# A delta-rule pipeline whose four hand-written step sequences are replaced by newly drawn ones

## The reference, cut to what matters

```
q = silu(dwconv_causal(x @ Wq)); k = silu(dwconv_causal(x @ Wk)); v = silu(dwconv_causal(x @ Wv))
alpha = sigmoid(x @ Wa + ba);   beta = sigmoid(x @ Wb + bb)
def step(S, inp):                       # over the 1024 tokens, for each batch and head
    qt, kt, vt, at, bt = inp
    err = einsum('bhvk,bhk->bhv', S, kt) - vt
    S = at[..., None, None] * S - bt[..., None, None] * err[..., None] * kt[:, :, None, :]
    o = einsum('bhvk,bhk->bhv', S, qt)
    return (S, o)
o = layernorm(o) * ln_w + ln_b;  o = o * sigmoid(x @ Wg);  return o @ Wo
```

## Time and profile before

| | us |
|---|---|
| median of 3 runs | 1928.25 |
| lowest, highest | 1923.27, 1929.74 |
| the profiled execution | 1926.59 |
| its span in the trace | 1924.9 |

### The profile page before, as it was taken

How to read it: one execution, slowest core, us unless ns; L and a number is a source line. 1 busy time by engine, 2 the same in 40 slices (tenths; PEclk the granted TensorE clock), 3 DMA queues, 4 the chain that set the end, 5 groups by cost and what they waited for, 6 DMA issues and landing times.

```text
span 1924.9 us, 49241 instructions
## 1 busy us (share of the span) xinstructions
PE 1815.8 (94%) x19366; PEld 1345.0 (70%) x19366; DVE 1472.8 (77%) x2561; ACT 1308.0 (68%) x2850; POOL 945.0 (49%) x1890
## 2 busy tenths in 40 slices
PE   8899999998999789999999999999999999999687
PEld 4633333333778678888888888888888888887576
DVE  6699999992665468788788788888887887886365
ACT  2078888887343367777777777777777777776453
POOL 1234454444223426566556656556656656655133
PEclk9989999999999989999999999999999999999789
DMA  5201212111000201111011011111111111111001
GB/s 181 82 18 34 58 33 58 33 47 23 12 1 6 70 24 46 37 43 54 24 49 48 27 45 48 35 44 41 35 48 38 35 48 38 37 37 46 4 1 44
DMA packets 74133, 78.61 MB, mean 41 GB/s; under 512 B 13168, under 2 KB 60784, under 8 KB 73904
## 3 DMA queue, kind: packets, MB, share of 16 engines
q1 hardware_dynamic: 73904, 75.46, 13.2%
HBM read 66.13 MB, written 8.91 MB: 39 GB/s over the span
## 4 chain that ended last, share of the span: by engine, by line
PE 33%; DVE 15%; POOL 14%; issue 5%; ACT 1%; POOLq 0%; DVEq 0%; ACTq 0%
PE ps L1530 9%; DVE d_acc L1834 7%; POOL d_inv L1485 6%; PE ps L1560 6%; POOL d_term L1478 6%; PE ps L1581 2%; PE ps L1649 2%; DVE d_lane L1865 2%; PE ps L1631 2%; PE ps L1679 2%; DVE d_r_sb L1886 1%; PE ps L2009 1%; PE ps L1655 1%; PE ps L2023 1%; DVE d_ap L1851 1%
## 5 line engine op out<-in xcount | busy, mean ns | idle before, releaser
L1834 DVE SCALAR_TENSOR_TENSOR d_acc<-ps,d_par,d_acc 128x1023 f32<-128x1023 f32 (+2 forms) x288 | 365.8, 1270 | 41.4 <-ACT d_acc L1702 41.1
L601 ACT ACTIVATE a_prob<-ps 128x512 f32<-128x512 f32 (+2 forms) x640 | 309.3, 563 | 96.4 <-PE ps L567 91.3
L1530 PE MATMUL ps<-x1p,d_wh 128*128 128x512 f32 x1024 | 352.6, 426 | 9.5 <-DVE d_acc L1834 6.7
L623 DVE TENSOR_REDUCE a_mx<-ps 128x2 f32<-128x1024 f32 (+2 forms) x320 | 336.5, 1111 | 32.6 <-PE ps L551 25.5
L1702 ACT ACTIVATE d_acc<-ps,d_par 128x512 f32<-128x512 f32 x192 | 149.3, 778 | 106.5 <-PE ps L1530 103.4
L1530 PE MATMUL ps<-x1p,d_wl 128*128 128x512 f32 x512 | 203.4, 397 | 0.0
L1530 PEld LDWEIGHTS ps<-x1p,d_wh 128*128 128x128 f32 x1024 | 168.4, 191 | 35.9 <-DVE d_acc L1834 16.3
L510 POOL TENSOR_SCALAR_AFFINE_SELECT a_prob<-a_prob 128x128 f32<-128x128 f32 (+1 forms) x384 | 125.2, 330 | 123.6 <-ACT a_prob L601 112.8
L567 PE MATMUL ps<-q,k 51*128 51x512 bf16 (+2 forms) x640 | 174.6, 363 | 2.7 <-ACT a_prob L601 0.9
L581 PE MATMUL ps<-a_prob,a_v 128*32 128x512 f32 (+3 forms) x1536 | 164.3, 500 | 0.4 <-POOL a_prob L510 0.2
L546 PE MATMUL ps<-k,q 48*128 48x512 bf16 (+3 forms) x768 | 150.2, 338 | 9.5 <-DVE a_mx L623 7.4
(11 more groups left out here) (244 smaller groups left out, 4553.3 us busy)
## 6 DMA issues: line engine op xcount, KB each, us to landing
d_abc<-scratch_alpha SPq DMA_DIRECT2D x32, 512.0 KB, 3.9
d_gb<-scratch_g SPq DMA_DIRECT2D x32, 512.0 KB, 4.3
d_wr<-in_dw SPq DMA_DIRECT2D x16, 512.0 KB, 3.6
scratch_q<-p_parts SPq DMA_DIRECT2D x24, 128.0 KB, 2.4
q<-scratch_q SPq DMA_DIRECT2D x32, 96.0 KB
scratch_y<-a_oT SPq DMA_DIRECT2D x64, 36.0 KB
x_tok<-in_x SPq DMA_DIRECT2D x4, 512.0 KB, 7.6
q<-scratch_q SPq DMA_DIRECT2D x32, 64.0 KB
```

The lines of the kernel that those rows point to most:

```text
L601: inc(nc.scalar.activation(prob[:, y % PB, g:g + heads, off:], ps[:, PLACE["st", n, x], 0:heads * w].rearrange("p (h c) -> p h c", c=w), A ...
L623: inc(nc.vector.tensor_reduce(out, ps[:, bank:bank + 2, 0:heads * w].rearrange("p r (h c) -> p r h c", c=w), AX.X, ALU.max, negate=True), ...
L1530: last = nc.tensor.matmul(ps[:, bank, :], wp[g][:, k, i, :], x(part), start=(k == 0 and j == 0), stop=(k == KE - 1 and j == 2))
L1834: inc(nc.vector.scalar_tensor_tensor(acc[i][:, d:T], taps[:, 0:T - d], par[p][:, 4 * i + j:4 * i + j + 1], acc[i][:, d:T], ALU.mult, ALU.a ...
```

## The change

Nothing is computed in another way, no instruction of the steady stage is added or removed, and buffers and banks are as they were. All four sequences of `ORDER` are new, in order and in where the stage is cut. Two waits are added in `last_layer`'s function for DVE, on adds that earlier rows of DVE's own sequence make.

```
 ORDER = {
     "PE": """
...
-        O.w.7 S.z64 O.qs.7 O.pw.7 X.out.1 L.proj.2.0.0 S.y128 L.proj.2.0.1 L.proj.2.1.0 L.proj.2.1.1 S.z128 L.pair.0 S.w.0 L.pair.1 S.s.0 L.pair.2
...
+        X.out.1 O.w.7 S.z64 O.qs.7 O.pw.7 L.proj.2.0.0 L.proj.2.0.1 L.proj.2.1.0 S.y128 L.proj.2.1.1 L.pair.0 S.z128 L.pair.1 S.w.0 S.gate.0.0 S.s.0
...
     "POOL": """
-        X.wo S.solve.0 S.solve.1 S.solve.2 S.solve.3 S.solve.4 X.og.0 L.split X.og.1 L.scalars O.stats L.qg""",
+        S.solve.2 S.solve.3 S.solve.4 X.og.0 S.qg X.og.1 L.scalars O.stats L.split O.wo L.solve.0 L.solve.1""",
 }
...
     def ahead_vector(dve, step):
         if step == ("o_turn", 0):
             waits(dve, "gproj", 2)
+            waits(dve, "added", -2)
             w_norm.statistics(dve, 0)
             w_norm.normalise(dve, 0)
         if step == ("out", 0):
             for k in range(KE):
                 dve.wait_ge(x_high, k + 1)
                 nc.vector.tensor_tensor(xp[:, 0, 1, k, :], ps[:, k, :], plain(xp[:, 0, 0, k, :]), ALU.subtract).then_inc(x_low, 1)
+            waits(dve, "added", 0)
             w_norm.statistics(dve, 1)
```

More of the change, by code:

```diff
@@ L1244 @@
     "PE": """
[L1245 to L1248, removed]
@@ L1249 @@
-        E.proj.0.1.1 S.s.2 L.k_turn.0 S.gate.1.0 S.gate.1.1 S.pw.2""",
+        O.qs.5 O.w.5 L.proj.1.1.0 O.s.5 L.proj.1.1.1 O.ks.6 O.pw.5 S.y32 S.v_turn.1 O.w.6 S.z32 X.out.0 O.qs.6 O.s.6 O.pw.6 S.y64 S.k_turn.1 O.ks.7
+        X.out.1 O.w.7 S.z64 O.qs.7 O.pw.7 L.proj.2.0.0 L.proj.2.0.1 L.proj.2.1.0 S.y128 L.proj.2.1.1 L.pair.0 S.z128 L.pair.1 S.w.0 S.gate.0.0 S.s.0
+        S.gate.0.1 S.ks.1 S.pw.0 L.pair.2 L.pair.3 S.w.1 S.qs.1 E.proj.0.0.0 S.s.1 E.proj.0.0.1 S.ks.2 S.pw.1 E.proj.0.1.0 S.w.2 E.proj.0.1.1 S.qs.2
@@ L1250 @@
+        S.s.2 X.out.2 S.pw.2 S.ks.3 O.o_turn.0 X.out.3 S.w.3 L.v_turn.0 S.qs.3 S.s.3 S.pw.3 S.gate.1.0 S.ks.4 S.gate.1.1 L.k_turn.0 S.w.4 S.qs.4
+        O.o_turn.1 S.s.4 S.pw.4 E.proj.1.0.0 S.ks.5 E.proj.1.0.1""",
     "ACT": """
-        X.norm.0 O.pw.0 O.w.1 X.o_turn.0 O.pw.1 S.blocks X.norm.1 O.w.2 L.tap.0.0 L.tap.0.1 S.silu.2 O.pw.2 O.gate.1 O.w.3 X.o_turn.1 O.pw.3
-        S.v_turn.0 S.v_turn.1 O.w.4 L.tap.1.0 O.pw.4 O.w.5 S.spread X.og.0 X.og.1 S.y32 L.tap.1.1 O.pw.5 O.w.6 S.diag S.y64 O.pw.6 O.w.7 S.gate.0
@@ L1253 @@
-        S.z64 O.pw.7 L.silu.0 L.silu.1 S.y128 L.tap.2.0 L.tap.2.1 S.z128 S.w.0""",
+        X.pw.6 X.w.7 O.z64 X.pw.7 S.silu.0 S.silu.1 S.tap.2.0 O.y128 S.tap.2.1 O.z128 O.w.0 X.norm.0 O.gate.0 O.pw.0 O.w.1 S.silu.2 S.blocks L.tap.0.0
+        O.pw.1 O.w.2 X.norm.1 L.tap.0.1 O.pw.2 X.o_turn.0 O.w.3 S.v_turn.0 O.pw.3 O.gate.1 O.w.4 O.pw.4 X.og.0 X.o_turn.1 O.w.5 L.tap.1.0 S.spread
+        L.tap.1.1 S.y32 O.pw.5 O.w.6 S.v_turn.1 X.og.1 S.diag S.y64""",
     "DVE": """
-        O.s.3 L.conv.0.2 O.ks.4 X.o_turn.0 O.s.4 S.columns O.pw.2 O.ks.5 X.o_turn.1 S.turned O.s.5 S.k_turn.1 O.ks.6 O.pw.3 S.whole L.conv.1.0 O.s.6
@@ L1256 @@
-        X.out.0 O.ks.7 L.conv.1.1 O.pw.4 L.conv.1.2 O.pw.5 O.pw.6 O.pw.7 X.out.1 O.stats L.decay L.conv.2.0 L.pair.0 S.s.0 L.pair.1 L.pair.2 S.ks.1
-        L.pair.3 L.conv.2.1 S.s.1 L.conv.2.2 S.ks.2 L.lanes S.pw.0 S.pw.1 X.out.2 X.out.3 S.s.2 L.k_turn.0 E.conv.0.0 S.ks.3 E.conv.0.1""",
+        X.o_turn.0 O.s.4 O.pw.2 O.pw.3 O.ks.5 O.pw.4 S.k_turn.0 S.columns O.s.5 O.ks.6 X.o_turn.1 S.turned L.conv.1.0 O.pw.5 S.whole X.out.0 O.s.6
+        L.conv.1.1 O.ks.7 L.conv.1.2 O.pw.6 X.out.1 O.pw.7 O.stats S.k_turn.1 L.decay L.pair.0 L.conv.2.0 L.pair.1 S.s.0 L.conv.2.1 S.ks.1 L.conv.2.2
@@ L1258 @@
+        L.pair.2 L.pair.3 S.s.1 S.ks.2 S.pw.0 L.lanes S.s.2 X.out.2 S.ks.3 E.conv.0.0 X.out.3 S.pw.1 S.s.3 E.conv.0.1 S.ks.4 E.conv.0.2""",
     "POOL": """
-        X.wo S.solve.0 S.solve.1 S.solve.2 S.solve.3 S.solve.4 X.og.0 L.split X.og.1 L.scalars O.stats L.qg""",
+        S.solve.2 S.solve.3 S.solve.4 X.og.0 S.qg X.og.1 L.scalars O.stats L.split O.wo L.solve.0 L.solve.1""",
 }
```

## The result

The kernel with the new order takes 1972.85 us (median of 4 runs, 1971.74 to 1976.33), the kernel before 1928.99 us (median of 4, 1923.27 to 1932.58) beside it. The ratio is 1.0233, with a 95% interval of 1.0205 to 1.0262: slower by 44 us. I had predicted 1919 us, 1902 to 1938. The direction and the range are both wrong.

A forecast was written before the change was run, and what follows sets the result against it. It took the chain of waits from lanes through columns to lanes as the bound, with only columns to lanes movable: 30 x (-0.3) + 0 for the ends = -9 us, giving 1919 us, range 1902 to 1938.

The forecast's parts named there:

- Edits that I cost at nothing: POOL's qg moved between the two og, loads of alpha and g reissued on SP, two added waits: all priced at 0.
- the case without cover: If nothing hid POOL's moved qg, it would cost its 2.4 us per period.
- Rival 2: Slower by ACT's queue, if y128's copies end later than C+14.6: period 35.9, +15, 1943 us; chance 0.18.
- C: The start of columns in a period, from which the prediction counts the times of its steps in us.
- the tap: On ACT, one tap now ahead of y128's copies costs 0.7 us and gives back the 0.6 gained before.
- The walk: Step-by-step sum of the new order from columns to lanes, durations kept: period 35.08 us against 35.38, 0.3 less.
- The blocks: ACT's four blocks ahead of lanes, hidden before, are no longer hidden and cost 1.7 us per period.
- over a microsecond: Sign expected in the new trace: DVE idle that long ahead of lanes until ACT's blocks end.
- The ceiling: Most a new order could gain on PE by matmul busy time: 0.17 us per period, 5 us in all; not used.
- rival 3: Much faster, if PE stalls that the walk does not name go too: period shorter by 1.4, -42, 1886 us; chance 0.08.
- Ends: Pipeline fill (-1) and drain (-1.4 and +2.1 to +2.6): together 0, give or take 3 us.
- the late gating: In the drain, DVE's second gating comes ahead of the low parts PE's first up waits for: +2.1 to +2.6 us.

The follow-up runs named there:

- experiment 1: The kernel with the new order, with POOL's qg moved from between the two og to behind the second: 1889.03 us, ratio 0.9814 to the kernel before.
- experiment 2: The kernel before with one step moved, POOL's qg placed right behind solve.4: 1930.84 us, ratio 1.0039 to the kernel before.

## Why the prediction was wrong, step by step

**The step that failed** is "Edits that I cost at nothing". I costed the move of qg at nothing, with 2.4 us per period if its covers were gone, and looked for cover in semaphores only: who waits for qg, and whether the solve does. Nobody waits for it. It costs DVE 2.0 us per period by shutting out its gating, and PE 1.0 more through the clock, together 3.0 where I had put 0. The figure that I gave for the case without cover was near by luck; it came about in a way that was not among my rivals. Rival 2 has the same sign, and y128's copies do end beyond its C+14.6 in the kernel after (C+16.28). But it hangs on ACT's queue and the tap: here the 3.0 us come from DVE and the clock, and in experiment 1 the same queue of ACT ends them at C+13.30.

**The walk** was too cautious from its first step on. Experiment 1 is the order without the stall, and the kernel after in the period that starts at 1154.47 is the order with it; times are behind C:

| step | predicted | experiment 1 | after |
|---|---|---|---|
| whole's second transpose ends | 5.05 | 4.45 | 6.45 |
| ym ends | 8.1 | 7.50 | 9.50 |
| z64's first copy starts | 9.05 | 8.32 | 11.31 |
| y128's copies end | 14.0 | 13.30 | 16.28 |
| w_sb of chunk 0 starts | 16.0 to 16.5 | 15.45 | 18.44 |
| first state | 17.0 to 17.5 | 16.38 | 19.36 |
| lanes | 23.0 to 23.4 | 22.33 | 25.32 |

In the first rows experiment 1 is 0.6 us ahead of my walk, and 0.7 to 1.1 us at lanes: y32 starts at C+1.23 there (1017.14), where I had taken C+1.7. I had credited the new order with whole coming 0.6 sooner, and it was 1.2. From there on the durations between steps are mine to within 0.2 us, lanes included. (The middle of my C+23.0 to C+23.4 is 23.2, and I wrote 23.25; that is 1.5 us over the pipeline and changes nothing.) The column of the kernel after shows the failure entering at once: 2.0 in the first two rows, 3.0 from the third on, once y64 and what stands behind it up to z64 have run at half clock.

**The blocks** are exposed as I had said: DVE waits 0.21 to 0.26 us for them ahead of lanes, after 0.58 for PE's ks. I had named "over a microsecond" as the sign, which was wrong, because a state and an r_sb fill the rest. The chain of the kernel after does not pass over line 1732 either; from 1170 to 1192 it lies on PE's own row. So does nearly all of experiment 1's chain from 1027 on, and PE's row is busy for 34.02 of its 34.24 us. The walk of copies and lanes followed a string that is close to PE's own but was not shown to be the one that binds; what sets the 34.24 us stays open.

**The ceiling.** I had said that by matmul busy time the order could gain 0.17 us per period at most, and rightly did not use that. The gain was 1.2. Weight loads fell from 29.58 to 28.95 us in a period, matmuls from 34.99 to 34.02. So rival 3, the large gain with 0.08 of chance (a period shorter by 1.4 us), is where the kernel would have been but for qg: by the ratio of experiment 1 to the 1928.25 us of before it is 1892 us, against its 1886.

**Ends.** I had 0, give or take 3. From the first projection to the first columns it is 39.0 us (38.1 before), and the first period 39.3 (40.1 before). The tail behind the last columns is 151.8 us (153.6 before): sum -1.6. Of the parts, the time from the first to the last statistics of the last layer, in which the late gating lies, grew by 2.7 us (1824.6 to 1859.1, now 1871.8 to 1909.0), where I had +2.1 to +2.6 for that gating; the statistics come 4.3 us sooner behind the last columns, which I had at 1.4. In experiment 1 they come 8.1 us sooner and the tail is 147.8 us.

## What to carry over

When an instruction on POOL or DVE is moved, list what runs at its new place on the other of the two, and from where each takes its inputs: in the pairs of a DVE and a POOL instruction shown here that both read two operands from SBUF (gating and qg, scan and eps, gating and solve), the later one got through only behind the earlier, with no semaphore to show it. In a trace the sign is a group whose maximum is far above its median, or a tiny instruction that takes microseconds and ends when one on the other engine ends; look for it before costing a move at nothing. Then price the stall from what stands behind it in the queue: 1.5 us cost nothing in 20 of 30 periods of one order (the mean of experiment 2 is 35.68 us against 35.46, and most of that lies in pauses of PE that the trace does not tie to the stall), and 2.0 us cost 3.0 in the other.
